# A graph attention pass on TensorE: block numbers from one register ring instead of two sets of loads

## The reference

```
xl = (x @ Wl + bl).reshape(n, heads, outc)
e_feat = jax.nn.leaky_relu(xl[src] + (x @ Wr + br).reshape(n, heads, outc)[dst], NEG_SLOPE)
logits = jnp.einsum('ehc,hc->eh', e_feat, att)
...
a = a / denom[dst]
out = jax.ops.segment_sum(xl[src] * a[:, :, None], dst, num_segments=n)
```

## Time and profile before

| | |
|---|---|
| time of the kernel before, median of 3 runs (lowest, highest) | 6167.75 us (6162.48, 6183.69) |
| the profiled execution, from its first to its last instruction | 8199.2 us |
| mean granted TensorE clock in it | 0.656 of full speed |
| POOL gathers of the first attention, L932 | 832 |
| POOL gathers of the three GAT passes, L1769 | 2496 |
| PE register loads of block numbers, L919 | 1407 |

### The profile page before, as it was taken

The page is one execution under the profiler, slowest core; times in us unless marked ns, Lnnn a source line. Parts: engine busy times, 40 slices in busy tenths (PEclk is TensorE's granted clock), DMA queues, the critical chain, the costliest instruction groups (busy, mean ns, idle before and its releaser), DMA issues. The chain is left out here.

```text
span 8199.2 us, 128493 instructions
## 1 busy us (share of the span) xinstructions
PE 5007.5 (61%) x25366; PEld 3730.4 (45%) x25375; DVE 4287.8 (52%) x10883; ACT 2730.0 (33%) x6600; POOL 3533.6 (43%) x3882
## 2 busy tenths in 40 slices
PE   2677777774888935555556345555555355655557
PEld 2555555553664524444444334444444244444443
DVE  6555555556664145555555545554556445555554
ACT  1333333333542003333334323333334133333342
POOL 2544444442320044555554445555552555555520
PEclk7676677776999965555556556555556555555568
DMA  2444444443444722222222122222221222222215
GB/s 72 128 137 135 137 134 139 134 137 86 134 134 158 249 54 58 64 62 62 65 59 61 42 54 63 62 59 66 60 63 35 54 60 61 60 60 61 58 35 202
DMA packets 579250, 728.81 MB, mean 89 GB/s; under 512 B 90091, under 2 KB 424769, under 8 KB 578686
## 3 DMA queue, kind: packets, MB, share of 16 engines
q0 software_dynamic: 123968, 282.81, 14.9%
q1 hardware_dynamic: 304800, 350.53, 14.5%
q10 hardware_dynamic: 149918, 88.82, 4.0%
HBM read 601.07 MB, written 120.75 MB: 88 GB/s over the span
## 5 line engine op out<-in xcount | busy, mean ns | idle before, releaser
L1769 POOL DMA_INDIRECT rows<-scratch_gat,index x2496 | 2437.4, 977 | 2757.1 <-DVE mix L1997 1461.9
L2103 PE MATMUL sums<-xr_part,hot_t 128*128 x7524 | 1106.9, 283 | 786.2 <-issue 466.9
L2158 PE MATMUL sums<-mix,vhot 128*128 128x128 f32 x4992 | 1261.8, 421 | 91.0 <-issue 81.7
L2103 PEld LDWEIGHTS sums<-xr_part,hot_t 128*128 128x128 bf16 x7524 | 775.5, 121 | 1102.7 <-issue 945.7
L2011 DVE TENSOR_TENSOR z<-sums,rows 128x512 f32<-128x512 f32 x624 | 428.7, 687 | 1563.0 <-remote 1425.4
L1836 ACT ACTIVATE moved_sums<-sums x624 | 373.1, 598 | 2620.8 <-remote 1599.0
L932 POOL DMA_INDIRECT rows<-scratch_kv,index_ring x832 | 820.6, 986 | 887.5 <-ACT index_ring L1242 661.3
L2158 PEld LDWEIGHTS sums<-mix,vhot 128*128 128x128 f32 x4992 | 1044.4, 303 | 186.6 <-issue 142.6
L1368 PE MATMUL sums<-at_hot,lo_hot 128*128 128x200 f32 x2496 | 820.1, 493 | 16.4 <-issue 11.2
L1826 ACT ACTIVATE vhot<-iota,edge_local 128x128 f32<-128x128 f32 x2496 | 791.2, 392 | 0.1
L2154 PE MATMUL sums<-zeros 128*128 128x8 bf16 x624 | 114.7, 184 | 999.9 <-issue 551.5
(11 more groups left out here) (514 smaller groups left out, 6385.9 us busy)
## 6 DMA issues: line engine op xcount, KB each, us to landing
piece<-scratch_adj SPq DMA_DIRECT2D x90, 1280.0 KB, 6.3
local_ring<-scratch_local_rows SPq DMA_DIRECT2D x633, 128.0 KB
scratch_spool<-rows ACTq DMA_DIRECT2D x208, 256.0 KB, 2.6
vals<-scratch_spool SPq DMA_DIRECT2D x208, 256.0 KB, 2.6
scratch_adj<-stage SPq DMA_DIRECT2D x25, 1600.0 KB
rows<-scratch_gat,index POOLq DMA_INDIRECT x2496
local_ring<-scratch_local_rows ACTq DMA_DIRECT2D x211, 128.0 KB
mask<-scratch_masks SPq DMA_DIRECT2D x234, 80.1 KB
```

The lines of the kernel that those rows point to most:

```text
L1769: eng.indirect_dma_start(rows[:, slot, q, k * LINE:(k + 1) * LINE], None, table, bass.IndirectOffsetOnAxis(ap=index[:, slot, s:s + 1], axis=0)
L2103: ins = eng.matmul(B.ps[:, at + k * D:at + (k + 1) * D], hot_t[:, slot, k * P:(k + 1) * P], part[:, bass.ds(at_block, D)], start=(j == 0), ...
L2158: ins = eng.matmul(B.ps[:, bass.ds(of_block * D, D)], hot[:, v % MIXES, k * P:(k + 1) * P], mix[:, v % MIXES, k * D:(k + 1) * D], start=Fa ...
```

## The change

On PE the two sets of registers (24 for asking, 24 for summing, and one for the first group) become one ring of 24. A group's block numbers are loaded once, for `ask`, into ring place n mod 24; `sum_up` thirteen steps after that load reads the same register through a copy (`held`). On ACT, in the first attention, the number `need` is worked out by a plain register operation into a register of its own.

```diff
+    def held(self, at):
+        return self.eng.snap(self.regs[at], min_val=0, max_val=(1 << 30) - 1)
...
+                need = eng.alloc_register(f"need{B.fresh()}")
...
-                            need = field(twos[0], NEED_FIELD.bit_length() - 1, 32, BLOCKS - 1)
-                            eng.wait_ge(room.sem, need + (room.at(0) + 1))
+                            eng.reg_alu(need, twos[0] // NEED_FIELD, 31, ALU.bitwise_and)
+                            eng.wait_ge(room.sem, eng.snap(need, min_val=0, max_val=BLOCKS - 1) + (room.at(0) + 1))
...
-                scored_blocks = [BlockRegisters(B, eng, PORTION_GROUPS) for h in range(RING_PORTIONS)]
-                summed_blocks = [BlockRegisters(B, eng, PORTION_GROUPS) for h in range(RING_PORTIONS)]
-
-                def ask(n, slot, blocks, four):
+                blocks = BlockRegisters(B, eng, RING_PORTIONS * PORTION_GROUPS)
+
+                def ask(n, slot, four):
...
+                    def ring_at(ahead):
+                        return (slot * PORTION_GROUPS + ahead) % (RING_PORTIONS * PORTION_GROUPS)
 
                     def load_blocks(q):
                         if scored and q < PORTION_GROUPS:
-                            next_of[q] = scored_blocks[slot].load(q, 1, p * PORTION_GROUPS + (q + 1))[0]
-                        if q in adding:
-                            sums_of[q] = summed_blocks[slot].load(q, 1, p * PORTION_GROUPS + (q - BEHIND))[0]
+                            next_of[q] = blocks.load(ring_at(q + 1), 1, p * PORTION_GROUPS + (q + 1))[0]
...
-                            sum_up((q - BEHIND) % PORTION_GROUPS, n - BEHIND, sums_of[q])
+                            sum_up((q - BEHIND) % PORTION_GROUPS, n - BEHIND, blocks.held(ring_at(q - BEHIND)))
```

More of the change, by code:

```diff
@@ L1295, in _ @@
                         keep(n, q)
-                for r in sum(regs, []):
+                for r in sum(regs, []) + [need]:
                     eng.free_register(r)
@@ L2165, in portion @@
                     adding = [q for q in range(PORTION_GROUPS) if summed(p, q, 0)]
-                    next_of, sums_of = {}, {}
+                    next_of = {}
+                    def ring_at(ahead):
+                        return (slot * PORTION_GROUPS + ahead) % (RING_PORTIONS * PORTION_GROUPS)
                     def load_blocks(q):
                         if scored and q < PORTION_GROUPS:
-                            next_of[q] = scored_blocks[slot].load(q, 1, p * PORTION_GROUPS + (q + 1))[0]
-                        if q in adding:
-                            sums_of[q] = summed_blocks[slot].load(q, 1, p * PORTION_GROUPS + (q - BEHIND))[0]
+                            next_of[q] = blocks.load(ring_at(q + 1), 1, p * PORTION_GROUPS + (q + 1))[0]
                     load_blocks(0)
@@ L2184, in portion @@
                             eng.wait_ge(zed.sem, zed.at(1) + n)
-                            ask(n + 1, (q + 1) % HOTS, scored_blocks[slot], next_of[q])
+                            ask(n + 1, (q + 1) % HOTS, next_of[q])
                         load_blocks(q + 1)
@@ L2192, in _ @@
                 eng.wait_ge(blank.sem, blank.at(1))
-                first = BlockRegisters(B, eng, 1)
                 with eng.Fori(0, 1):
-                    ask(0, 0, first, first.load(0, 1, 0)[0])
+                    ask(0, 0, blocks.load(0, 1, 0)[0])
                 run_portions(eng, portion)
-                for regs in scored_blocks + summed_blocks + [first]:
-                    regs.free()
+                blocks.free()
                 end.tensor(eng)
```

## The result

| | |
|---|---|
| time after, median of 17 runs (lowest, highest) | 6187.26 us (6168.12, 6200.56) |
| time before, 17 runs on the same chip | 6170.91 us (6151.45, 6183.69) |
| ratio after to before | 1.0029, interval 1.0018 to 1.0039 |
| the profiled execution of after | 6174.35 us, span 6172.5 us |

The change makes the kernel slower by 0.29%, some 16 us, where the sum of the prediction gave plus 2 and the forecast minus 3.

The account below looks back on a forecast made before the run. The prediction took POOL's gathers to bound the GAT passes and a ring of PE and ACT the first attention. Its terms gave 6168 - 6 + 8 = 6170 us, no change; it put the time at 6165, range 6050 to 6195.

Parts of the forecast that it names:

- That is recording, not work.: GAT passes: PE's lateness in the profile, 7.4 us a group mid-pass against 4.55 without gathers, was laid to recording.
- to about 7990: Profiled execution: span expected to fall from 8199 us to this, as PE isn't covered there; the runs nowhere near that.
- the pace of the chain: PE, DVE, ACT in the passes: 4.55 us a group, 0.5 to spare under POOL's gathers at 5.05.
- The gathers bound the passes.: GAT passes in the runs: stand on POOL's gathers, 1.26 us each, 5.05 a group, with nothing to spare.
- One load fewer: covered.: PE in the passes: 0.36 us a group, 226 us of queue time, goes but is hidden under the gathers.
- Changes no start of a gather.: GAT passes: PE 0.36 us a group shorter leaves every gather's start as it was, 0 us.
- Minus 6 for the ends of the passes.: Twelve groups of sums after each pass's gathers: the removed load saves 0 to 4 us a pass, 2 taken.
- Plus 8 for `need` on ACT.: First attention, ACT queue: added register operations cost 0 to 0.15 us a pair, 0.08 taken, over 104 pairs.
- DVE's z is last anyway: First attention: reason for the lower bound of 0 us a pair on the cost of `need` on ACT.
- the chain as bound: Rival, passes: PE, DVE, ACT bound the runs too; 6056 us, or 5942 at full price; chance 0.24.
- the ends of the passes: Rival: 12 groups at 0.76 us three times save 27 us, giving 6141, faster by 0.4%; chance 0.08.
- the ACT ring: Rival, first attention: two more instructions on PE's waiting path, deciding from 0.18 us a pair; 6190 us, slower; chance 0.16.

Follow-up runs that it names:

- after_fourth: The whole change against before, on a chip where before takes 8028 us: 8029.97 us, 0.9999.
- act_only_again: Before with only the edit of `need` on ACT, both PE loads in place, lower level: 6177.34 us, 1.0019 of before.
- after_load3: Changed kernel meant to have three more PE loads a group; the program got one short register operation a group instead: 6185.98 us, 1.0034 of before.
- both_moved_again: Changed kernel with ACT's table load, `need` and wait for room moved behind the first group's one-hot, lower level: 6125.95 us, 0.9935 of before.
- both_late: Changed kernel with table load, `need`, wait for room, wait for z and index copy all behind the pair's first one-hot: 6126.16 us, 0.9938 of before.
- act_heavy_again: Before with the ACT edit's operations written five times; the repeats aren't in the program, so only the ACT edit, lower level: 6169.39 us, 1.0005 of before.
- act_moved_again: Before with the ACT edit, and table load, `need` and wait for room behind the one-hot, lower level: 6109.74 us, 0.991 of before.
- after_again: The changed kernel once more, lower level: 6175.6 us, 1.0021 of before.
- act_only: Before with only the edit of `need` on ACT in the first attention, upper level: 8211.74 us, 0.9999 of before.
- act_chain: Before with the ACT edit and eight dependent steps more per pair ahead of the wait for room, upper level: 8101.24 us, 1.0084 of before.

## Why the prediction was wrong, by its steps

**"That is recording, not work."** Wrong, as above: the span of after is 6172.5 beside a time of 6174.35. The span that fell "to about 7990" rested on it, and the whole change at the upper level came out at 0.9999 (after_fourth), not 209 us lower. So did the pace of the chain. The prediction took the eight groups behind the last gather as clean, 36.37 us or 4.55 a group. At the lower level the same eight groups take 27.5 to 27.7 us in act_only_again, 3.44 a group. So the clean portion was slowed too, and the chain had 1.8 us a group to spare under gathers of 5.2, not 0.5.

**The gathers bound the passes.** Right at the lower level. 2449 of the 2496 gathers follow the one before after 0.3 us, and DVE waits for rows. The forecast interval was 1.258 to 1.276 and the trace has 1.307, because a gather's mean is 1.002 us and not its median of 0.958. That the balance closed was luck: the first attention took 1194 us and not the 1215 I gave it, and what lies outside the four phases 6172.5 - 1193.8 - 3258.7 = 1720 and not 1928 - 111 = 1817. These two were 118 us too long together and the passes 123 too short.

**One load fewer: covered.** Right that it brings nothing. Some of the saved time shows up as waiting: DVE's wait for gathered rows is 466 to 477 us in the three traces at this level with both loads and 516 to 527 in the six without the second, while POOL's wait for mix stays at 12 to 16. The group of gathers of act_only_again (count, busy us, mean ns, idle before and what ended it):

```profile
L1770 POOL DMA_INDIRECT rows<-scratch_gat,index x2496 | 2484.0, 995 | 1338.6 <-issue 746.8 <-DVEq L1905 578.7 <-DVE mix L1998 13.1
```

And of after:

```profile
L1773 POOL DMA_INDIRECT rows<-scratch_gat,index x2496 | 2501.5, 1002 | 1339.3 <-issue 746.8 <-DVEq L1908 579.2 <-DVE mix L2001 13.4
```

**"Changes no start of a gather."** This is the step that failed: the term for PE's load under the gathers, put at 0, with a gain able only to be hidden. The two rows have the same idle time, to 0.7 us, and 17.5 us more busy: with the ring the gathers themselves take longer. That pair is the widest. Gathers are busy 2496.8 to 2501.5 us in the six traces at the lower level whose PE has the ring (after three times, after_load3, both_moved_again, both_late; mean 2498.4), and 2484.0 to 2491.8 in the three whose PE is as before (act_only_again, act_heavy_again, act_moved_again; mean 2487.9): 10.5 us, and no overlap. On one chip the difference is 13 to 16, on another 5 to 9. The three phases, first to last gather, come to 3253 to 3259 us against 3241 to 3249. Each trace is one execution, and there are nine.

What stretches them is open. The medians are alike (955 to 958 ns), so most of it is in the long ones: 299 to 329 gathers take over 1.1 us with the ring, 270 to 281 without. One thing that goes with a long gather can be read from the same traces: in after the 872 gathers with one of DVE's `mix` operations beside them have a mean of 1038 ns and the other 1624 one of 983. That doesn't explain the change, though. The gathers beside a `mix` are as many with the ring (837 to 872) as without (843 to 853), and those without a `mix` are longer with it by 3 to 5 ns in the mean too. The kernels that were to test whether it comes from PE's shorter queue had no load added, and the higher clock of PE in these kernels wasn't separated from it either.

**Minus 6 for the ends of the passes.** Too large. Outside the gather phases, from the first pass's last gather on (two gaps between passes and the tail), six traces with the ring have 496.3 to 500.8 us (mean 498.6) and three without 498.2 to 502.4 (mean 500.3): 1.7 us less for 36 groups, with ranges that overlap, so 2 or nothing. The eight groups behind a last gather take 27.2 to 29.3 us in after and after_again, and 27.5 to 27.7 in act_only_again, where ACT's one-hot and DVE's softmax end the steps, as said.

**Plus 8 for `need` on ACT.** Right in size. The edit alone was 11.6 us above before in one set (6177.34 to 6165.75) and 8.6 in the other (6169.39 to 6160.78); by the means of the runs 11.3 and 4.8, 8 together, with a standard error of 2, so 4 to 12. The traces say the same of the place. By source line, one pair of before at the upper level: the register load, then the index copy.

```profile
L1272 ACTq TENSOR_LOAD <-adj_evac_table x1: 1211/1211/1211, 1211.8 to 1211.8; - x1
...
L1242 ACT ACTIVATE index_ring<-edge_src x1: 210/210/210, 1213.4 to 1213.4; 128x8 int32 x1
```

The same of act_only, at the same level:

```profile
L1273 ACTq TENSOR_LOAD <-adj_evac_table x1: 1192/1192/1192, 1215.3 to 1215.3; - x1
...
L1242 ACT ACTIVATE index_ring<-edge_src x1: 209/209/209, 1216.9 to 1216.9; 128x8 int32 x1
```

1.6 us both times, with a load 19 ns shorter in the second; the rows are rounded to 0.1 us. The unrounded starts of the same two pairs, quoted in the expectation of act_heavy_again, give 0.408 us from the load's end to the copy in before and 0.488 in act_only. Over all 104 pairs the medians are 0.395 in before and 0.465 or 0.466 in the traces with the edit, at both levels; the means differ by 0.07 to 0.08, the 0.08 of the prediction. And the bound of 0 for "DVE's z is last anyway" falls: in before no pair takes over 0.6 us from load to copy, so neither the wait for room nor that for z holds ACT there, and the same is true of after and act_only_again. In after the fused operation of 0.126 us is two of 0.048 at L1278:

```profile
L1278 ACTq ALU_OP  x208: 38/48/73, 199.3 to 1403.1; - x104
```

Behind them stands a fused one at L1279:

```profile
L1279 ACTq FUSED_REGOPS  x104: 41/47/47, 199.5 to 1403.1; - x104
```

2 x 0.048 + 0.047 = 0.143 against 0.126 is 0.02 busy, and the rest of 0.08 is the gaps of two more instructions. That this queue is on the path was shown at the upper level, where seven to eight tenths of an added delay arrive (act_chain twice), and by the move, which brings 132 us there and 51 at the lower. At the lower level no added delay was measured. The edit itself cost nothing at the upper level that its three runs could tell (0.9999, 0.9997, 0.9996); each interval is 11 to 15 us wide to either side and takes in the 6 or 7 us that were due. There the table's load is also shorter with the edit, 1.13 us in the mean against 1.17, so that from its start to the copy a pair takes only 0.03 to 0.04 us more than in before, 4 us in all. Whether the load is shorter through the edit isn't shown.

**The sum.** 8 from ACT, 10.5 from longer gathers, less 2 at the ends: 16 to 17 us, and the result has 16. The prediction's own terms make 2, so the term that it lacked is the gathers'. That the sum meets the result so closely is in part luck, as the two repeats at this level had 10 and 7 by the medians and 12 and 9 by the means. By times alone PE's part is less sure than by the traces. After less act_only is -1.7 and -1.8 us in the two sets by the medians, 0.7 and 4.4 by the means, and the pair with the moved wait gives 12, each with a standard error of 4 to 5; together 5, with one of 2.5. The first attention alone varies by more than the whole effect between traces of one kernel (1190.7, 1193.8 and 1218.9 us in three of after). ACT's 8 is shown by the edit alone; for PE the times allow anything from 0 to 10, and the traces say 9.

**"I put it at 6165, as gains that I can't see in PE are likelier than losses."** A lean on nothing in the profile, in the wrong direction: all three sets at this level have after above before. Of the rivals, the chain as bound is refuted by POOL's row of waits, the ends of the passes by the 1.7 us, and the ACT ring stands with the price of the main case, 0.08 us a pair, not with the 0.18 from which it was to decide. The forecast's own signs misled in one point: the span fell by 2027 us and not by 200, and the runs didn't follow, because it was the level that fell.

## What to carry to other kernels

Compare the span of a profile with its own execution's time and with the level of the runs before any argument on what recording costs: here the profile came from a level a third above that of the runs, and the same program at the other level has another bound.

A stage that stands on POOL's gathers brought nothing for the 226 us of queue time saved on PE, and the 8 us of register operations on ACT stayed. Look for what stands ahead of a one-hot or an index copy in the queue: moving the table load and its wait behind them was worth 51 us where the change cost 16.

An experiment that adds work must be looked up in its own trace before it is believed: three kernels here had lost what they were to add; in each of them nothing read it.

## What the hardware showed that I had not expected

- The same program took 6161 to 6171 us in three sets and 8028 to 8204 us in the three others. At the upper level PE's register operations of 32 ns take up to 1405, and PEld waits 936.1 us for issue at L2104. Register moves and operations of over 0.4 us are found on PE and SyncE by the hundred there, and on no engine at the lower level.
- At that level one added register operation of 0.032 us a group on PE (576 at its line) went with a kernel 46 us under after and, in the next set, 53 us under before; at the lower level it was 10 us above after.
- Gathers beside a PE stream with fewer loads are 10.5 us longer in 2496, with equal gaps between them. A gather with one of DVE's `mix` operations beside it has a mean of 1038 ns in after, against 983.
- With the second load gone TensorE's granted clock was 0.727 to 0.738 in place of 0.710 to 0.723, in every run at the lower level whose clock is on record, and the time was no shorter.
